# Who writes the final mask: VectorE before the hand-over, or ScalarE in front of each exponential

## The chip, the cores and the metric

One core of a Trainium2 chip runs the whole program. The metric is device time in microseconds of one execution; the kernel before took 3034.04 us (median of 3 runs, 3031.94 to 3041.01).

## The reference, cut to what matters

Four layers run one after the other on 2048 tokens of 128 features: linear attention, a mixture-of-experts feed-forward, the talking-heads attention that this change touches, and a second mixture of experts. The third layer, with 16 heads, 16 memory slots ahead of the 2048 keys, and a causal mask:

```python
dots = jnp.einsum('bhid,bhjd->bhij', q, k) * SCALE
dots = jnp.einsum('bhij,hk->bkij', dots, pre_proj)
dots = jnp.where(causal, NEG_INF, dots)
topk_vals = jax.lax.top_k(dots, K)[0]          # K = 64
thresh = topk_vals[..., -1:]
dots = jnp.where(dots < thresh, NEG_INF, dots)
attn = jax.nn.softmax(dots, axis=-1)
out = jnp.einsum('bhij,bhjd->bhid', attn, v)
```

Each row of scores keeps its 64 largest entries, all others get the weight zero.

## The kernel before, in words

The attention works on 64 groups `k`. A group is one tile of 128 queries (`t = k // 4`, 16 tiles) with four heads (`GU = 4`). Its rows are `n = 16 + 128 * (t + 1)` wide: 144 columns in the first four groups, 2064 in the last four. Scores stand in `S[:, k % 3, i, 0:n]`, in a ring of three groups (`NS = 3`), the mask in `F[:, i, 0:n]`, of which there is one copy only. Every engine runs its own list of instructions in order, and they meet at semaphores.

**VectorE**, per group: `pivots(k)` merges sorted lists to a pivot that lies close to the threshold (24 small operations and, beside them, `list_step(k + 1, ...)`, 64 MAX8 over the scores of the next group, L1106, four in each of 16 steps of `beside`), computes `negm` and `cutb` and raises `s_cut`. Then comes `memory_weights(k - 1)`, which waits for the exponentials of the group before and writes `Pm` from `F` and `S` (L1260). Then `below(k, i)` for four heads (L1155, L1157), and `threshold(k)`: it waits for ScalarE's counts (`s_cnt`), makes the threshold `thr`, judges whether a row is doubtful (L1228 to L1248), writes the masks of the four heads between these small steps (`mask`, L1176: 4.0 where the score lies below the threshold), reads the flag, skips the exact settlement `settle` in almost all groups, and raises `s_lose`. Before the first mask it waits until TensorE has read the masks of the group before (`s_tfill`, L1233).

**ScalarE**, in round `p`: `exponent(p - 1, i)` for four heads, in place in `S` (L543, waits for `s_lose`); the drains `drain_turn` of the first three transposed blocks (L550, a Relu from PSUM); `count_above(p, i)` for four heads (L536, waits for `s_cut`), with one further `drain_turn` behind each; the remaining `drain_turn`; `drain_rest(p - 1)`; and last `drain_scores(p + 2)`, which copies the scores of the group after next out of PSUM (L521). The exponentials of group `p` stand behind these copies in the list.

**TensorE**, in round `p`: `outputs(p - 2)`, `values(p - 1)` and `group_scores(p + 2)`. In `values`, `turn` transposes each block of exponentials (L807, waits for `s_prob` of its head) and subtracts the transposed mask in the same place of PSUM (L808); the Relu of the drain turns the difference into zero where the mask stands. `turn_memory` (L816) waits for `Pm`; `product` (L823) multiplies with the values.

```python
for p in range(NG):
    pivots(p)
    if p >= 1:
        memory_weights(p - 1)
    for i in range(GU):
        below(p, i)
    threshold(p)
```

Of the kernel before, what the change touches and what calls it, by code (L numbers as in the profile page):

```python
# [5 lines left out]
ALU = mybir.AluOpType  # L6
ACT = mybir.ActivationFunctionType
# [16 lines left out]
NS = 3  # L24
SC = 1024
BIG_ = 2.0 ** 90
# [7 lines left out]
GU = 4  # L34
# [11 lines left out]
def wide(t):  # L46

    return MEM + P * (t + 1)
# [114 lines left out]
def build(nc, out, x, Wqkv, bqkv, wi, bi, wo, bo0, loraA, loraB, gate_w, gate_b, Wq, Wkv, Wo, bo1, pre, mem_k, mem_v,  # L163
          ln_w, ln_b, router_w, gw1, uw1, dw1, shg, shu, shd):
    fills, ffills = plan_fills(), plan_ffn1()
    with ExitStack() as ctx:
# [3 lines left out]
        def sem(name):  # L170
            return ctx.enter_context(nc.semaphore(name))
# [27 lines left out]
        thr = sb("thr", [P, GU])  # L199
# [21 lines left out]
        sm = sb("sm", [P, 8, NT])  # L221
# [44 lines left out]
        WvZ = SA[:, 13184:15232].rearrange("p (c e n) -> p c e n", c=8, e=2)  # L266
        mvZ = SA[:, 15232:16256].rearrange("p (c e m) -> p c e m", c=8, e=2)
        mkS = SA[:, 2048:4096].rearrange("p (c k m) -> p c k m", c=8, k=H1)
        S = R[:, 0:NS * GU * WIDE].rearrange("p (r i n) -> p r i n", r=NS, i=GU)
        A = R[:, NS * GU * WIDE:(NS * GU + 2) * WIDE].rearrange("p (r n) -> p r n", r=2)  # L270
        F = sb("F", [P, GU, WIDE], BF16)
# [21 lines left out]
        s_dve = sem("s_dve")  # L293
# [21 lines left out]
        s_eight = sem("s_eight")  # L315
        s_lose = sem("s_lose")
        s_prob = sem("s_prob")
        s_pm = sem("s_pm")
        s_tfill, s_tdrain = sem("s_tfill"), sem("s_tdrain")
        s_pv = sem("s_pv")  # L320
# [13 lines left out]
        def turned(k):  # L334
            return turn_of["p", k, k // 4] + 1
# [77 lines left out]
        def _(act):  # L413
# [48 lines left out]
            n = fills.index("loraA_gate")  # L462
# [75 lines left out]

            def exponent(k, i):
                n = wide(k // 4)  # L540
                act.wait_ge(s_lose, k + 1)
                row = S[:, k % NS, i, 0:n]
                act.activation(row, row, ACT.Exp, bias=negm[:, k % 2, i:i + 1], scale=1.0 / LOW).then_inc(s_prob, 1)  # L543

            def drain_turn(k, j):
# [52 lines left out]
            for e in range(E0 + 1):  # L598
                for b in range(4):
                    for i in range(2):  # L600
                        k = (e * 4 + b) * 2 + i
# [320 lines left out]
        def _(dve):  # L922
            done = [0]

            def mark(ins):
                done[0] += 1
                ins.then_inc(s_dve, 1)
# [39 lines left out]
            for b in range(4):  # L967
                k = drained(("q", b))
# [11 lines left out]
            k = drained("kvsum")  # L980
# [21 lines left out]
            k = drained("logit0")  # L1002
# [93 lines left out]
            def list_step(k, first, count):  # L1096

                if k >= NG:
                    return  # L1100
                n = wide(k // 4)
                for m in range(first, first + count):
                    i, c = divmod(m, CH)
                    if c == 0:
                        dve.wait_ge(s_sdrain, last_slot(k, i) + 1)
                    mark(dve.max(cand[:, :, c, i], lists(S[:, k % NS, i, 0:n], n, c)))  # L1106

            def pivots(k):

                def beside(step, ins):
                    mark(ins)
                    stage = done[0]
                    list_step(k + 1, 4 * step, 4)
                    dve.wait_ge(s_dve, stage)
                    return step + 1

                dve.wait_ge(s_dve, done[0])
                mark(dve.tensor_reduce(top[:, :], cand[:, 0].rearrange("p l u -> p u l"), AX.X, ALU.max))  # L1119
                link(dve.tensor_scalar(W16[:, 0, :], cand[:, :, :, :].rearrange("p r l u -> p (r l u)"), 1.0 / LOW, -RANGE,  # L1120
                                       ALU.mult, ALU.max))
                flip, runs, step = 0, 8, 0
                while runs < TOPK:
                    inner = 8 * CH * GU // (2 * runs)
                    src = W16[:, flip, :].rearrange("p (r h n) -> p r h n", r=runs, h=2)
                    flip = 1 - flip
                    dst = W16[:, flip, :].rearrange("p (h r n) -> p h r n", h=2, r=runs)
                    mark(dve.tensor_tensor(dst[:, 0], src[:, :, 0, :], src[:, ::-1, 1, :], ALU.max))
                    step = beside(step, dve.tensor_tensor(dst[:, 1], src[:, :, 0, :], src[:, ::-1, 1, :], ALU.min))
                    d = runs // 2  # L1130
                    while d:
                        src = W16[:, flip, :].rearrange("p (r h n) -> p r h n", h=2, n=d * inner)
                        flip = 1 - flip
                        dst = W16[:, flip, :].rearrange("p (r h n) -> p r h n", h=2, n=d * inner)
                        mark(dve.tensor_tensor(dst[:, :, 0, :], src[:, :, 0, :], src[:, :, 1, :], ALU.max))  # L1135
                        step = beside(step, dve.tensor_tensor(dst[:, :, 1, :], src[:, :, 0, :], src[:, :, 1, :], ALU.min))  # L1136
                        d //= 2
                    runs *= 2
                src = W16[:, flip, :].rearrange("p (r h u) -> p r h u", h=2, u=GU)
                dst = W16[:, 1 - flip, 0:CUT * GU].rearrange("p (r u) -> p r u", u=GU)  # L1140
                beside(step, dve.tensor_tensor(dst, src[:, 0:CUT, 0, :], src[:, CUT - 1::-1, 1, :], ALU.max))
                link(dve.tensor_reduce(piv[:, :], dst.rearrange("p r u -> p u r"), AX.X, ALU.min))
                mark(dve.tensor_scalar(negm[:, k % 2, :], top[:, :], -1.0 / LOW, None, ALU.mult))
                link(dve.tensor_scalar(cutt[:, :], piv[:, :], -BIG_ * LOW * (1 - NEAR), BIG_ * LOW * SLACK,
                                       ALU.mult, ALU.add))
                link(dve.scalar_tensor_tensor(out=cutb[:, k % 2, :], in0=piv[:, :], scalar=-BIG_ * LOW * (1 + NEAR),
                                              in1=cutt[:, :], op0=ALU.mult, op1=ALU.max))
                dve.sem_inc(s_cut, 1)  # L1148
# [22 lines left out]
                                                in1=bob[:, 0:P - 1] if g == 0 and i == 0 else y, op0=ALU.mult,  # L1171
                                                op1=ALU.add)

            def mask(k, i):
                n = wide(k // 4)
                mark(dve.tensor_scalar(F[:, i, 0:n], S[:, k % NS, i, 0:n], thr[:, i:i + 1], 4.0, ALU.is_lt, ALU.mult))  # L1176

            def settle(k, i):

                n = wide(k // 4)  # L1180
                dve.tensor_reduce(doubts[:, 0, 0:1], doubt[:, i::GU], AX.X, ALU.max)
                dve.drain()
                dve.transpose(doubts[:, 1, :], doubts[:, 0, :])
                dve.drain()
                dve.tensor_reduce(flag[:, :], doubts[0:1, 1, :], AX.X, ALU.max)
                dve.drain()
                row, rest, m_ = S[:, k % NS, i, 0:n], A[:, 1, 0:n], r9[:, i, 1:9]
                with dve.If(dve.value_load(flag[0:1, 0:1], min_val=0, max_val=1) != 0):
                    for r in range(8):
                        dve.max(m_, rest if r else row)  # L1190
                        dve.drain()
                        if r < 7:
                            dve.match_replace(rest, m_, rest if r else row, 2 * FILL)
                            dve.drain()
                    dve.tensor_copy(thr[:, i:i + 1], m_[:, 7:8])
                    dve.drain()
                    dve.tensor_scalar(F[:, i, 0:n], row, thr[:, i:i + 1], 4.0, ALU.is_lt, ALU.mult)
                    dve.drain()

            def threshold(k):  # L1200
# [27 lines left out]
                    mark(dve.scalar_tensor_tensor(out=doubt[:, GU * g:GU * g + GU], in0=th[rows_g, :], scalar=0.0,  # L1228
                                                  in1=tie[rows_g, :], op0=ALU.is_equal, op1=ALU.max))
                judged = done[0]  # L1230
                if k:

                    dve.wait_ge(s_tfill, turned(k - 1))  # L1233
                mask(k, 0)
                dve.wait_ge(s_dve, judged)
                mark(dve.tensor_reduce(doubts[:, 0, 0:1], doubt[:, :], AX.X, ALU.max))
                judged = done[0]
                mask(k, 1)
                dve.wait_ge(s_dve, judged)
                mark(dve.transpose(doubts[:, 1, :], doubts[:, 0, :]))  # L1240
                judged = done[0]
                mask(k, 2)
                dve.wait_ge(s_dve, judged)
                mark(dve.tensor_reduce(flag[:, :], doubts[0:1, 1, :], AX.X, ALU.max))
                judged = done[0]
                mask(k, 3)
                dve.wait_ge(s_dve, judged)
                doubtful = dve.value_load(flag[0:1, 0:1], min_val=0, max_val=1)  # L1248
                with dve.If(doubtful != 0):
                    dve.drain()  # L1250
                    for i in range(GU):
                        settle(k, i)
                dve.wait_ge(s_dve, done[0])
                dve.sem_inc(s_lose, 1)  # L1254

            def memory_weights(k):
                dve.wait_ge(s_prob, GU * k + GU)
                if k:
                    dve.wait_ge(s_tfill, turn_of["m", k - 1, 0] + 1)
                dve.scalar_tensor_tensor(out=Pm[:, :, :], in0=F[:, :, 0:MEM], scalar=1.0, in1=S[:, k % NS, :, 0:MEM],  # L1260
                                         op0=ALU.is_lt, op1=ALU.mult).then_inc(s_pm, 1)

            list_step(0, 0, CH * GU)
            for p in range(NG):
                pivots(p)
                if p >= 1:
                    memory_weights(p - 1)
                for i in range(GU):
                    below(p, i)
                threshold(p)  # L1270
# [80 lines left out]
```

## Time and profile before

| | us | share of the span |
|---|---|---|
| median of the runs shown | 3034.04 | |
| profiled execution | 3029.58 | |
| its span | 3027.1 | |
| VectorE busy | 2415.8 | 80% |
| TensorE busy (matmul) | 2302.1 | 76% |
| ScalarE busy | 1414.6 | 47% |
| the 64 groups of attention, first pivot to the end of the last products | some 2440 | 81% |

The profile shows one execution. Busy times are shares of the whole span, over stages that differ: before 325 us and after 2770 us other layers run. Inside the attention the groups grow from 20.5 us at the start to about 54 us at the end, so what an operation costs has to be read by stretch. "Idle before" is the time in which an engine stood still ahead of a group of instructions, with the instruction that released it; "issue" is a pause for which the profile shows no releaser. DVE is VectorE, ACT is ScalarE, PE is TensorE.

### The profile page before, as it was taken

How to read it: one execution, taken by the hardware profiler on the slowest of the kernel's cores; microseconds unless marked ns; L12 is line 12 of the kernel's file. 1: busy time of each engine (PE TensorE's matmuls, PEld its weight loads, DVE VectorE, ACT ScalarE, POOL GpSimd, SP SyncE). 2: the span in 40 equal slices, each digit the busy share in tenths (PEclk: the TensorE clock that was granted, in tenths of full speed). 3: DMA queues.
4: the chain of work that ended last, by engine and by line, in shares of the span. 5: the costliest groups of instructions: out<-in, count | busy, mean ns of one | idle time of the engine just before them, and what ended most of it. 6: DMA issues, size and time to landing. Idle time of an engine off the chain costs nothing.

```text
span 3027.1 us, 34365 instructions
## 1 busy us (share of the span) xinstructions
PE 2302.1 (76%) x10182; PEld 1328.8 (44%) x10182; DVE 2415.8 (80%) x9392; ACT 1414.6 (47%) x2143; POOL 5.2 (0%) x43
## 2 busy tenths in 40 slices
PE   6696545657767757778888888988984888884897
PEld 3554323333434424444444444544542545442564
DVE  2506688889888988989899999999998988884445
ACT  1121223444445435555565666666663666652221
POOL 0000000000000000000000000000000000000000
PEclk7798667777878878899998999999997999987898
DMA  2000000000000000000000000000000000001000
GB/s 59 1 0 1 1 1 1 1 1 1 2 1 1 1 1 1 1 1 1 1 1 1 1 1 1 1 1 1 1 1 1 1 1 1 1 1 49 1 1 14
DMA packets 15509, 12.20 MB, mean 4 GB/s; under 512 B 6892, under 2 KB 13686, under 8 KB 15222
## 3 DMA queue, kind: packets, MB, share of 16 engines
q1 hardware_dynamic: 11184, 6.82, 0.9%
q10 hardware_dynamic: 4038, 2.37, 0.3%
q14 instruction: 206, 1.69, 0.2%
q8 instruction: 81, 1.33, 0.2%
HBM read 8.14 MB, written 1.05 MB: 3 GB/s over the span
## 4 chain that ended last, share of the span: by engine, by line
DVE 53%; PE 30%; ACT 8%; issue 7%; DVEq 2%; ACTq 0%
DVE cand L1106 13%; DVE R L1155 7%; DVE r L1157 7%; PE bank L823 6%; PE bank L791 6%; PE bank L903 4%; DVE W L1136 4%; DVE F L1176 4%; DVE W L1135 4%; ACT R L543 4%; PE bank L807 3%; ACT R L536 3%; PE bank L911 2%; DVE WP L1170 2%; PE bank L808 1%
## 5 line engine op out<-in xcount | busy, mean ns | idle before, releaser
L823 PE MATMUL bank<-WP,Y 128*128 128x512 f32 x1088 | 685.4, 718 | 152.0 <-ACT WP L550 151.2
L807 PE MATMUL bank<-ident,R 128*128 128x128 f32 x2176 | 524.0, 315 | 248.8 <-ACT R L543 246.6
L1106 DVE MAX8 cand<-R 128x8 f32<-128x12 f32 (+15 forms) x4096 | 642.6, 226 | 5.3 <-ACT R L521 4.2
L791 PE MATMUL bank<-hT,qT 128*128 128x512 f32 (+3 forms) x1280 | 533.1, 555 | 37.3 <-ACT R L521 22.2
L807 PEld LDWEIGHTS bank<-ident,R 128*128 128x128 f32 x2176 | 346.2, 159 | 465.6 <-issue 214.7
L550 ACT ACTIVATE WP<-bank 128x512 f32<-128x512 f32 x544 | 320.8, 594 | 369.8 <-PE bank L808 368.6
L808 PE MATMUL bank<-nidentb,F 128*128 128x128 bf16 x2176 | 466.3, 240 | 0.0
L536 ACT ACTIVATE R<-R,cutb 128x144 f32<-128x144 f32 (+15 forms) x256 | 310.2, 1212 | 294.1 <-DVEq L1148 292.5
L521 ACT ACTIVATE R<-bank 128x1024 f32<-128x1024 f32 (+7 forms) x384 | 290.5, 774 | 278.6 <-PE bank L791 168.3
L1155 DVE SCALAR_TENSOR_TENSOR R<-R,r 128x144 f32<-128x144 f32 (+15 forms) x256 | 350.3, 1368 | 9.2 <-DVE r L1154 0.2
L543 ACT ACTIVATE R<-R,negm 128x144 f32<-128x144 f32 (+15 forms) x256 | 289.8, 1205 | 123.9 <-DVEq L1254 123.7
L791 PEld LDWEIGHTS bank<-hT,qT 128*128 128x128 f32 x1280 | 232.2, 198 | 262.3 <-issue 191.8
L1157 DVE MAX8 r<-R 128x8 f32<-128x144 f32 (+15 forms) x256 | 335.8, 1312 | 8.8
L808 PEld LDWEIGHTS bank<-nidentb,F 128*128 128x128 bf16 x2176 | 257.1, 118 | 142.9 <-issue 142.9
L823 PEld LDWEIGHTS bank<-WP,Y 128*128 128x128 f32 x1088 | 192.4, 221 | 205.7 <-ACT WP L550 194.4
L1136 DVE TENSOR_TENSOR W<-W 128x256 f16<-128x256 f16 x768 | 220.4, 287 | 0.0
L1176 DVE TENSOR_SCALAR F<-R,thr 128x144 bf16<-128x144 f32 (+15 forms) x256 | 196.9, 770 | 27.1 <-PE bank L808 25.3
L1135 DVE TENSOR_TENSOR W<-W 128x256 f16<-128x256 f16 x768 | 211.9, 276 | 1.2 <-DVE cand L1106 0.8
L1119 DVE TENSOR_REDUCE top<-cand 128x4 f32<-128x64 f32 x64 | 17.2, 269 | 128.6 <-issue 118.0
L816 PE MATMUL bank<-ident,Pm 128*64 128x128 f32 x64 | 20.3, 317 | 130.9 <-DVE Pm L1260 130.9
L903 PE MATMUL bank<-R 128*128 128x512 f32 x256 | 115.1, 593 | 0.7 <-ACT R L587 0.7
L587 ACT ACTIVATE R<-bank 128x512 f32<-128x512 f32 x76 | 45.4, 597 | 144.4 <-PE bank L903 140.2
(225 smaller groups left out, 2164.1 us busy)
## 6 DMA issues: line engine op xcount, KB each, us to landing
R<-in_L_attn_Wkv ACTq DMA_DIRECT2D x2, 512.0 KB, 8.0
R<-in_L_ffn_gate_w SPq DMA_DIRECT2D x1, 1024.0 KB, 7.7
R<-in_L_ffn_up_w SPq DMA_DIRECT2D x1, 1024.0 KB, 10.3
out<-X SPq DMA_DIRECT2D x1, 1024.0 KB, 5.1
R<-in_L_attn_Wq ACTq DMA_DIRECT2D x1, 512.0 KB, 6.1
WP<-in_L_attn_Wo ACTq DMA_DIRECT2D x1, 512.0 KB, 10.5
R<-in_L_ffn_wi SPq DMA_DIRECT2D x1, 256.0 KB
R<-in_L_ffn_wo SPq DMA_DIRECT2D x1, 256.0 KB
```

The lines of the kernel that those rows point to most:

```text
L536: act.activation(A[:, 0, 0:n], S[:, k % NS, i, 0:n], ACT.Sign, bias=cutb[:, k % 2, i:i + 1], scale=BIG_, accum_out=cnt[:, k % 2, i:i + 1]) ...
L543: act.activation(row, row, ACT.Exp, bias=negm[:, k % 2, i:i + 1], scale=1.0 / LOW).then_inc(s_prob, 1)
L550: act.activation(PT[:, b % 4, :], bank[4 + n % 2], ACT.Relu).then_inc(s_tdrain, 1)
L791: last = pe.matmul(to, qT[:, k % 2, i, :], hT[:, a:b], start=True, stop=b < n, skip_group_check=True)
L807: pe.transpose(to[:, P * i:P * i + P], S[:, k % NS, i, blk], ident[:, :])
L808: last = pe.matmul(to[:, P * i:P * i + P], F[:, i, blk], nidentb[:, :], start=False, stop=True, skip_group_check=True)
L823: pe.matmul(bank[6], Y[:, j, :], PT[:, (blocks_before(k) + j) % 4, :], start=(j == 0), stop=(j == k // 4))\
L1106: mark(dve.max(cand[:, :, c, i], lists(S[:, k % NS, i, 0:n], n, c)))
L1135: mark(dve.tensor_tensor(dst[:, :, 0, :], src[:, :, 0, :], src[:, :, 1, :], ALU.max))
L1136: step = beside(step, dve.tensor_tensor(dst[:, :, 1, :], src[:, :, 0, :], src[:, :, 1, :], ALU.min))
L1155: link(dve.scalar_tensor_tensor(out=A[:, 1, 0:n], in0=row, scalar=r9[:, i, 0:1], in1=row, op0=ALU.is_gt, op1=ALU.subtract, reverse1=True))
L1157: dve.max(r9[:, i, 1:9], A[:, 1, 0:n]).then_inc(s_eight, 1)
```

## The change

VectorE no longer writes the masks. It keeps the small steps of the judgement, and at the end of `threshold` writes the four thresholds times 2^90 into `thrb`, in one of two halves. ScalarE gets a second activation per head in `exponent`: a Relu over the whole row, with that threshold as bias and -2^90 as scale, so that `F` is zero where the score reaches the threshold and very large where it doesn't. It waits for its own Relu (`s_mask`), since the exponential overwrites the row that the Relu reads. Ahead of the first head it waits for `s_pm` and for TensorE's reading of the old masks. `memory_weights(k - 1)` moves from behind `pivots(k)` into it: step 7 in groups below 8, one step later every eight groups, step 14 of the 16 (0 to 15) from group 56 on. The exact settlement no longer rewrites its mask.

```diff
             def exponent(k, i):
                 n = wide(k // 4)
-                act.wait_ge(s_lose, k + 1)
                 row = S[:, k % NS, i, 0:n]
+                if i == 0:
+                    act.wait_ge(s_lose, k + 1)
+                    if k:
+                        act.wait_ge(s_pm, k)
+                        act.wait_ge(s_tfill, turned(k - 1))
+                act.activation(F[:, i, 0:n], row, ACT.Relu, bias=thrb[:, k % 2, i:i + 1], scale=-BIG_).then_inc(s_mask, 1)
+                act.wait_ge(s_mask, GU * k + i + 1)
                 act.activation(row, row, ACT.Exp, bias=negm[:, k % 2, i:i + 1], scale=1.0 / LOW).then_inc(s_prob, 1)
...
                     list_step(k + 1, 4 * step, 4)
+                    if k >= 1 and step == 7 + k // 8:
+                        memory_weights(k - 1)
                     dve.wait_ge(s_dve, stage)
...
-            def mask(k, i):
-                n = wide(k // 4)
-                mark(dve.tensor_scalar(F[:, i, 0:n], S[:, k % NS, i, 0:n], thr[:, i:i + 1], 4.0, ALU.is_lt, ALU.mult))
...
                     dve.tensor_copy(thr[:, i:i + 1], m_[:, 7:8])
-                    dve.drain()
-                    dve.tensor_scalar(F[:, i, 0:n], row, thr[:, i:i + 1], 4.0, ALU.is_lt, ALU.mult)
                     dve.drain()
...
                 judged = done[0]
-                if k:
-
-                    dve.wait_ge(s_tfill, turned(k - 1))
-                mask(k, 0)
                 dve.wait_ge(s_dve, judged)
                 mark(dve.tensor_reduce(doubts[:, 0, 0:1], doubt[:, :], AX.X, ALU.max))
                 judged = done[0]
-                mask(k, 1)
...
-                dve.wait_ge(s_dve, done[0])
-                dve.sem_inc(s_lose, 1)
+                dve.tensor_scalar(thrb[:, k % 2, :], thr[:, :], BIG_, None, ALU.mult).then_inc(s_lose, 1)
...
                 pivots(p)
-                if p >= 1:
-                    memory_weights(p - 1)
                 for i in range(GU):
                     below(p, i)
```

## Rows read from the trace of the kernel before

**Rows 1.** The page: busy time by engine, and two rows of the 40 slices.

```profile
PE 2302.1 (76%) x10182; PEld 1328.8 (44%) x10182; DVE 2415.8 (80%) x9392; ACT 1414.6 (47%) x2143; POOL 5.2 (0%) x43
PE   6696545657767757778888888988984888884897
DVE  2506688889888988989899999999998988884445
```

**Rows 2.** Groups by line, 1174 to 2770 us: mean ns, then idle before and releaser.

```profile
L807 PE MATMUL bank<-ident,R 128*128 128x128 f32 x1728 | 397.6, 305 | 158.4 <-ACT R L543 157.4
L536 ACT ACTIVATE R<-R,cutb 128x1168 f32<-128x1168 f32 (+8 forms) x140 | 223.6, 1597 | 62.5 <-DVEq L1148 62.5
L543 ACT ACTIVATE R<-R,negm 128x1040 f32<-128x1040 f32 (+8 forms) x144 | 216.6, 1580 | 35.2 <-DVEq L1254 35.1
L1176 DVE TENSOR_SCALAR F<-R,thr 128x1168 bf16<-128x1168 f32 (+8 forms) x140 | 141.4, 1011 | 26.1 <-PE bank L808 25.3
L816 PE MATMUL bank<-ident,Pm 128*64 128x128 f32 x36 | 9.8, 273 | 0.0
```

**Rows 3.** Groups by line, 325 to 1174 us.

```profile
L536 ACT ACTIVATE R<-R,cutb 128x144 f32<-128x144 f32 (+7 forms) x116 | 86.6, 746 | 231.6 <-DVEq L1148 229.9
L543 ACT ACTIVATE R<-R,negm 128x144 f32<-128x144 f32 (+6 forms) x112 | 73.1, 723 | 88.6 <-DVEq L1254 88.6
L1176 DVE TENSOR_SCALAR F<-R,thr 128x144 bf16<-128x144 f32 (+7 forms) x116 | 55.5, 479 | 0.9
L816 PE MATMUL bank<-ident,Pm 128*64 128x128 f32 x28 | 10.4, 373 | 130.9 <-DVE Pm L1260 130.9
```

**Rows 4.** Chain that ended last, in order of time: start us, us, what.

```profile
2589.59 7.73 ACT R L543 x4
...
2642.74 7.73 ACT R L543 x4
```

**Rows 5.** Timeline of ScalarE, group 60: start, us, instruction, idle before.

```profile
2588.67 1.02 ACT L521 ACTIVATE R<-bank 128x1024 f32<-128x1024 f32 x1 [0.75 <-PE bank L793]
...
2597.98 0.60 ACT L550 ACTIVATE WP<-bank 128x512 f32<-128x512 f32 x1 [0.67 <-PE bank L808]
```

**Rows 6.** Timeline of TensorE: behind the late settlement, and beside rows 5.

```profile
2327.17 0.45 PE L807 MATMUL bank<-ident,R 128*128 128x128 f32 x1 [28.11 <-ACT R L543]
...
2335.46 0.27 PE L807 MATMUL bank<-ident,R 128*128 128x128 f32 x1
...
2591.74 0.30 PE L807 MATMUL bank<-ident,R 128*128 128x128 f32 x1 [0.97 <-ACT R L543]
...
2595.46 0.48 PE L807 MATMUL bank<-ident,R 128*128 128x128 f32 x1 [1.52 <-ACT R L543]
...
2597.36 0.47 PE L807 MATMUL bank<-ident,R 128*128 128x128 f32 x1 [1.32 <-ACT R L543]
...
2599.02 2.02 PE L823 MATMUL bank<-WP,Y 128*128 128x512 f32 x2
...
2601.84 1.08 PE L823 MATMUL bank<-WP,Y 128*128 128x512 f32 x2
```

**Rows 7.** Timeline of ScalarE, groups 9 and 10.

```profile
570.48 2.19 ACT L543 ACTIVATE R<-R,negm 128x400 f32<-128x400 f32 x4 [5.75 <-DVEq L1254]
...
583.89 0.63 ACT L536 ACTIVATE R<-R,cutb 128x400 f32<-128x400 f32 x1 [5.64 <-DVEq L1148]
```

**Rows 8.** Timeline of VectorE, groups 60 and 61.

```profile
2571.05 1.29 DVE L1176 TENSOR_SCALAR F<-R,thr 128x2064 bf16<-128x2064 f32 x1 [4.43 <-PE bank L808]
...
2578.77 0.27 DVE L1119 TENSOR_REDUCE top<-cand 128x4 f32<-128x64 f32 x1 [2.56 <-issue]
...
2598.56 0.16 DVE L1144 TENSOR_SCALAR cutt<-piv 128x4 f32<-128x4 f32 x1
2598.76 0.16 DVE L1146 SCALAR_TENSOR_TENSOR cutb<-piv,cutt 128x4 f32<-128x4 f32 x1
```

**Rows 9.** Groups by line, whole span: the loads of ScalarE's tables at L428.

```profile
L428 ACT ACT_TABLE_LOAD x5 | 6.4, 1283 | 14.2 <-issue 14.1
```

More of the change, by code:

```diff
@@ L268, in build @@
         mkS = SA[:, 2048:4096].rearrange("p (c k m) -> p c k m", c=8, k=H1)
+        thrb = sm[:, 0, 0:2 * GU].rearrange("p (a i) -> p a i", a=2)
         S = R[:, 0:NS * GU * WIDE].rearrange("p (r i n) -> p r i n", r=NS, i=GU)
@@ L317, in build @@
         s_prob = sem("s_prob")
+        s_mask = sem("s_mask")
         s_pm = sem("s_pm")
@@ L1241, in threshold @@
                 judged = done[0]
-                mask(k, 2)
                 dve.wait_ge(s_dve, judged)
@@ L1245, in threshold @@
                 judged = done[0]
-                mask(k, 3)
                 dve.wait_ge(s_dve, judged)
```

## The prediction

> **What bounds the kernel now.** I read the page first. Overall VectorE is busy 80%, TensorE 76% and ScalarE 47%; in the slices VectorE stands at 8 or 9 tenths through the whole attention, and TensorE climbs beside it from 5 to 8 and 9 [rows 1]. By these shares VectorE is the bound and ScalarE has room. That reading is true for the first half only. What decides is who waits for whom, by stretch.
>
> In the early stretch (325 to 1174 us, groups 0 to 28) ScalarE stands idle 88.6 us ahead of its exponentials until VectorE raises `s_lose`, and 231.6 us ahead of its counts until VectorE raises `s_cut`; VectorE waits for nobody ahead of its masks (0.9 us in all), and TensorE waits 130.9 us for `Pm` [rows 3]. VectorE sets the pace.
>
> In the late stretch (1174 to 2770 us, groups 29 to 63) it turns round. TensorE waits 157.4 us for the exponentials and not at all for `Pm`. ScalarE's wait for `s_cut` has shrunk to 62.5 us, its wait for `s_lose` to 35.1 us, and VectorE waits 25.3 us for TensorE ahead of its masks [rows 2]. The timeline of group 60 shows why: ScalarE's last copy of scores starts at 2588.67 and takes 1.02 us, and the four exponentials follow with no gap at all, 2589.59 to 2597.32, although VectorE had been done with the masks for more than ten microseconds (its next pivot started at 2578.77) [rows 4, 5, 8]. TensorE meanwhile does one transposition per finished exponential and waits again, and gets going only behind the fourth, at 2597.36 [rows 6]. The chain that ended last holds these pieces of four exponentials, 7.73 us each, with 53.15 us from one to the next [rows 4]. So late groups run in a serial ring: exponentials on ScalarE, transpositions, products and new scores on TensorE, their copies on ScalarE, next exponentials. VectorE runs beside that ring.
>
> **The change, part by part.**
>
> *Relu on ScalarE, late stretch.* It is put exactly into that ring, in front of each exponential, and TensorE has nothing else in its list to do meanwhile. The trace has no Relu of this shape. The nearest row is the exponential over the same rows with the same kind of bias; the count, another function over the same rows, has nearly the same mean (1597 against 1580 ns), so I take the exponential's busy time again: 216.6 us for 144 activations [rows 2]. The wait on its own semaphore takes away the overlap of neighbours. Four exponentials of 400 columns take 2.19 us back to back, about 0.52 us apart; a count of the same width takes 0.63 us [rows 7]. A start behind a wait for the end of such an activation comes at 0.63 and a little, so about 0.13 us later than without, and 144 of them add 18.7 us. Bounds of that gap: zero, if the overlap stays, to 0.20, the whole distance of two dependent small operations on VectorE [rows 8]; that is 0 to 29 us. Added to the ring: 235 us.
>
> Not all of it lengthens the ring, since the ring has slack that it would use up first. ScalarE's 62.5 us of waiting for `s_cut` [rows 2] is time in which the ring waited for VectorE. With longer groups the pivots are there earlier. But `memory_weights(k - 1)` now stands inside `pivots(k)` and waits for the last exponential of the group before, and behind it come one to six further steps and the tail of `pivots`: in group 61 `pivots` takes 20.1 us from L1119 to L1146 for 16 steps and its tail [rows 8], so one step and the tail come to some 3 us, and four to six of the shorter steps of narrower groups to some 6. ScalarE first has three blocks to drain in that time, which TensorE hands over until about 2602, some 5 us behind the last exponential [rows 6]. I leave 8 us of the wait standing and take 54 as absorbed. Of the 35.1 us behind `s_lose`, most stands at one group with a settlement on VectorE, behind which TensorE had paused 28.11 us [rows 6], and the remaining 7 or so at the end; by my reading the first shrinks by about 6, since VectorE is further ahead of the ring, and the second goes: 13 absorbed. Late stretch: 235 - 54 - 13 = +168 us.
>
> *Masks off VectorE.* Late, it saves 141.4 us of busy time and 25.3 us of waiting [rows 2], and I cost both at nothing, since the ring doesn't wait for VectorE there. What then hides VectorE is the ring; VectorE will wait at L1260. Early, the saving counts. But of four masks three stood between the small steps of the judgement and hid their latencies. Now these are bare: three steps at 0.20 us, the distance of two dependent small operations [rows 8], and about 0.05 for the new `thrb`, 0.65 us per group. The reading of the flag behind the last step took longer than the fourth mask before and stays as it is. So 29 groups save three quarters of 55.5 [rows 3] = 41.6, less 29 x 0.65 = 18.9, which is 22.8. I choose to give the last five of them nothing (5 x 1.5 = 7.5 us less), since the ring takes over just behind them and grows earlier than before. Early stretch: -15 us.
>
> *Relu on ScalarE, early.* 73.1 + 112 x 0.13 = 88 us more work lies beside VectorE's; cover is the 231.6 and 88.6 us that ScalarE stood idle [rows 3]. *`memory_weights` moved.* The same instruction, 0.23 us, once per group; TensorE's 130.9 us of waiting for `Pm` [rows 3] mostly goes, and is worth nothing while VectorE sets the pace. What it can cost: behind L1260 are queued the rest of `pivots`, `s_cut`, and so ScalarE's counts. Early, four pairs take 8 x 0.72 = 5.8 us in the mean [rows 3], and the step comes at the middle of `pivots`, so I cost the wait at nothing; if it came 1 us too late in each of 29 groups, 29 us. *ScalarE's new waits* for `s_pm` and `s_tfill` are met already, because its own drains of the group before stood behind the same events: nothing. *The settlement* without its four masks: two groups, under 5 us.
>
> *The pause ahead of L1119.* The 2.56 us of "issue" stand behind the branch over the settlement [rows 8]. The block gets a little shorter; whether more or fewer groups pay, the trace doesn't tell. I keep it, with 20 us either way.
>
> *A rule of the skill.* The masks take 1011 ns on VectorE where an activation over the same rows takes 1580 [rows 2], so the work grows by more than half as it moves. The Trainium skill, "ScalarE: Activation LUTs", Rules for kernel authors, says to use VectorE, not ScalarE, for relu, since VectorE is up to about three times faster per element in bf16. It speaks against this change; here the input is f32, and the trace gives a ratio of 1.6. By a factor of three the estimate for the late masks would be 424 us instead of 235; the row decides.
>
> **The sum.** 168 - 15 = +153 us on the profiled execution of 3029.6 us, which gives 3183. The median of the runs shown is 4.5 us higher, and I put the forecast at 3185 us.
>
> **The rivals.**
>
> *VectorE bounds throughout, the masks' going is a gain.* For it: the slices show VectorE at 9 tenths to the end [rows 1]. Then three quarters of all masks, 0.75 x 196.9 = 148, less 64 x 0.65 = 42, and the 25 us of waiting go: 131 us faster, 2903 us. It decides from the point where the exponentials start on `s_lose` and not behind ScalarE's copies. Against it: no gap ahead of the exponentials of group 60 [rows 4, 5], and only 35.1 us of waiting for `s_lose` in 144 exponentials [rows 2].
>
> *The ring's slack is larger than I read.* TensorE might make up the delay, since fewer of its turns would meet the counts on ScalarE. If half of the 168 us were made up, the time is 3100. A case within 0.3% would need all of it.
>
> *The change doesn't do what it says:* Relu and exponential would reload tables between them. A load takes 1.28 us [rows 9]; eight per group make over 600 us. But the drains' Relu at L550 follows the last exponential after 0.67 us, a wait for TensorE and no load [rows 5]. 1%.
>
> **Chances.** Forecast 72%; slack larger 10%; clock 8%; VectorE bound 6%; about no change 3%; tables 1%. The range runs from 3105 to 3250: it takes in the bounds of the self-wait, the pause and most of the slack. About 0.3% is what a measurement of this kernel can tell from no change. Faster by over 0.3%: 0.07; within: 0.03; slower: 0.90.
>
> **What would show it.** Right: in late groups the four pairs of Relu and exponential take 16 us on ScalarE, directly behind L521; TensorE's idle ahead of L807 grows from 158 to about 370 us; VectorE's busy time falls by about 190 us and it stands waiting at L1260; the late groups take some 60 us. Early groups get up to 1 us shorter. Wrong: if late exponentials start on `s_lose`, if the Relu takes clearly more or less than the exponential, or if the part of the ring that isn't exponentials (45 us in group 60) changes.

## The result, and the profile after

The changed kernel takes 3160.15 us (median of 4 runs, 3156.91 to 3162.37) against 3034.38 us before (median of 4 runs): a ratio of 1.041, 95% interval 1.0391 to 1.0429. It is 126 us slower. The profiled execution has a span of 3159.0 us against 3027.1.

The overview page of the changed kernel: busy time by engine, and two rows of the 40 slices, answering to [rows 1].

```profile
PE 2303.4 (73%) x10182; PEld 1332.7 (42%) x10182; DVE 2254.5 (71%) x9198; ACT 1719.4 (54%) x2399; POOL 5.2 (0%) x43
PE   6697555667777577777777877878685778765797
...
DVE  2406688888988888878787877777679776763445
```

VectorE has lost 161 us of busy time and ScalarE has gained 305. TensorE's busy time is the same, spread over a longer span. VectorE no longer stands at 9 tenths towards the end but at 6 and 7: it is the engine that waits now.

Where the time went is told by two stretches with the same 29 and 35 groups as before. Groups by line of the changed kernel, 325 to 1153 us (groups 0 to 28), answering to [rows 3]; the columns are busy us, mean ns of one, idle time before and its releaser:

```profile
L815 PE MATMUL bank<-ident,R 128*128 128x128 f32 x448 | 130.5, 356 | 147.7 <-ACT R L551 147.7
L538 ACT ACTIVATE R<-R,cutb 128x144 f32<-128x144 f32 (+7 forms) x116 | 86.6, 747 | 130.4 <-DVEq L1158 128.8
L549 ACT ACTIVATE F<-R,sm 128x144 bf16<-128x144 f32 (+6 forms) x112 | 81.0, 723 | 67.1 <-DVE sm L1250 67.1
L824 PE MATMUL bank<-ident,Pm 128*64 128x128 f32 x28 | 8.6, 305 | 11.8 <-DVE Pm L1256 11.7
```

L549 is the new Relu, L551 the exponential, L538 the count, L1250 the new `thrb` (a part of the tile `sm`, under whose name it stands in the views), L1256 the memory weights. `DVEq L1158` is VectorE's raising of `s_cut`. ScalarE still waits for VectorE here, only less. The first pivot of group 29 starts 815.5 us behind that of group 0; before it was 844.8. The early stretch has gained 29 us.

The same view from 1153 to 2905 us (groups 29 to 63), answering to [rows 2]:

```profile
L815 PE MATMUL bank<-ident,R 128*128 128x128 f32 x1728 | 402.4, 308 | 370.2 <-ACT R L551 370.2
L551 ACT ACTIVATE R<-R,negm 128x1040 f32<-128x1040 f32 (+8 forms) x144 | 228.7, 1588 | 4.7
L549 ACT ACTIVATE F<-R,sm 128x1040 bf16<-128x1040 f32 (+8 forms) x144 | 226.9, 1576 | 23.5 <-DVE sm L1250 23.5
L538 ACT ACTIVATE R<-R,cutb 128x1168 f32<-128x1168 f32 (+8 forms) x140 | 223.8, 1599 | 3.4 <-DVEq L1158 3.3
L824 PE MATMUL bank<-ident,Pm 128*64 128x128 f32 x36 | 9.8, 273 | 0.0
L1256 DVE SCALAR_TENSOR_TENSOR Pm<-F,R 128x64 f32<-128x64 bf16 x36 | 8.0, 224 | 247.3 <-ACT R L551 247.3
```

TensorE's wait for exponentials has grown from 158 to 370 us. ScalarE's wait for `s_cut` ahead of its counts has gone from 62.5 to 3.4 us: the ring has used up its slack. And VectorE stands still for 247.3 us ahead of the memory weights. That large number is a symptom. VectorE waits because the ring is longer, and the experiments below show that its place in the list costs nothing here (`mask_only`), as long as it stands late enough in the pivots (`step7`).

One late group in order of time. Timeline of ScalarE in group 59 of the changed kernel (start us, duration, instruction; in brackets idle before), answering to [rows 5]:

```profile
2636.11 1.02 ACT L523 ACTIVATE R<-bank 128x1024 f32<-128x1024 f32 x1 [0.75 <-PE bank L801]
2637.03 1.90 ACT L549 ACTIVATE F<-R,sm 128x1936 bf16<-128x1936 f32 x1
2638.96 1.91 ACT L551 ACTIVATE R<-R,negm 128x1936 f32<-128x1936 f32 x1
2640.78 1.89 ACT L549 ACTIVATE F<-R,sm 128x1936 bf16<-128x1936 f32 x1
...
2650.18 1.91 ACT L551 ACTIVATE R<-R,negm 128x1936 f32<-128x1936 f32 x1
```

TensorE beside it, answering to [rows 6]:

```profile
2641.02 0.30 PE L815 MATMUL bank<-ident,R 128*128 128x128 f32 x1 [2.80 <-ACT R L551]
2644.66 0.47 PE L815 MATMUL bank<-ident,R 128*128 128x128 f32 x1 [3.29 <-ACT R L551]
...
2652.14 0.47 PE L815 MATMUL bank<-ident,R 128*128 128x128 f32 x1 [3.16 <-ACT R L551]
...
2653.80 1.74 PE L831 MATMUL bank<-WP,Y 128*128 128x512 f32 x2
2655.38 0.27 PE L815 MATMUL bank<-ident,R 128*128 128x128 f32 x1
```

And VectorE: the thresholds are handed over at 2619.41, 18 us before ScalarE looks at them, and then it waits at L1256 for the last exponential, which ends at 2652.09.

```profile
2619.41 0.17 DVE L1250 TENSOR_SCALAR sm<-thr 128x4 f32<-128x4 f32 x1 [3.52 <-issue]
...
2652.12 0.23 DVE L1256 SCALAR_TENSOR_TENSOR Pm<-F,R 128x64 f32<-128x64 bf16 x1 [9.59 <-ACT R L551]
```

The block in front of TensorE lasts from 2637.03 to 2652.09, 15.1 us; in the kernel before the same group took 7.3 us, and its pieces stand in the chain that ended last (start us, us, what):

```profile
2536.75 7.30 ACT R L543 x4
...
2589.59 7.73 ACT R L543 x4
```

From the end of that block to the start of the next it took 2589.59 - 2544.05 = 45.5 us before. The same chain of the changed kernel has the first Relu of group 60 at 2696.75, 44.7 us behind 2652.09:

```profile
2696.75 2.02 ACT F L549
```

So in this group the rest of the ring is nearly what it was, and the block in it has doubled.

### The profile page after: what moved, and what is told of

It reads as the page before. It is cut to its first block, busy times and chain, and to the rows that moved or that the text cites. A ratio compares the mean times of both kernels' runs of the same rounds, so it can differ in the third digit from the quotient of the medians.

```text
span 3159.0 us, 34424 instructions
## 1 busy us (share of the span) xinstructions
PE 2303.4 (73%) x10182; PEld 1332.7 (42%) x10182; DVE 2254.5 (71%) x9198; ACT 1719.4 (54%) x2399; POOL 5.2 (0%) x43
## 4 chain that ended last, share of the span: by engine, by line
PE 42%; DVE 29%; ACT 21%; issue 7%; DVEq 2%; ACTq 0%
PE bank L799 10%; PE bank L831 10%; ACT R L551 7%; DVE cand L1114 7%; ACT F L549 7%; PE bank L815 5%; PE bank L911 4%; ACT R L538 4%; DVE R L1165 3%; DVE r L1167 3%; DVE W L1146 2%; PE bank L816 2%; ACT R L523 2%; DVE W L1145 2%; PE bank L919 2%
## 5 line engine op out<-in xcount | busy, mean ns | idle before, releaser
L815 PE MATMUL bank<-ident,R 128*128 128x128 f32 x2176 | 532.9, 318 | 517.9 <-ACT R L551 517.9
L831 PE MATMUL bank<-WP,Y 128*128 128x512 f32 x1088 | 653.9, 688 | 55.3 <-ACT WP L558 53.5
L799 PE MATMUL bank<-hT,qT 128*128 128x512 f32 (+3 forms) x1280 | 540.2, 559 | 115.0 <-ACT R L519 91.2
L523 ACT ACTIVATE R<-bank 128x1024 f32<-128x1024 f32 (+7 forms) x384 | 290.5, 774 | 286.4 <-PE bank L799 168.3
L538 ACT ACTIVATE R<-R,cutb 128x144 f32<-128x144 f32 (+15 forms) x256 | 310.5, 1213 | 133.8 <-DVEq L1158 132.0
L549 ACT ACTIVATE F<-R,sm 128x144 bf16<-128x144 f32 (+15 forms) x256 | 307.9, 1203 | 90.6 <-DVE sm L1250 90.6
L551 ACT ACTIVATE R<-R,negm 128x144 f32<-128x144 f32 (+15 forms) x256 | 311.0, 1215 | 8.3
L831 PEld LDWEIGHTS bank<-WP,Y 128*128 128x128 f32 x1088 | 184.0, 212 | 108.1 <-ACT WP L558 97.0
L1146 DVE TENSOR_TENSOR W<-W 128x256 f16<-128x256 f16 x768 | 216.5, 282 | 0.8 <-issue 0.8
L1145 DVE TENSOR_TENSOR W<-W 128x256 f16<-128x256 f16 x768 | 209.0, 272 | 0.4
L1256 DVE SCALAR_TENSOR_TENSOR Pm<-F,R 128x64 f32<-128x64 bf16 x64 | 13.7, 215 | 247.3 <-ACT R L551 247.3
L1250 DVE TENSOR_SCALAR sm<-thr 128x4 f32<-128x4 f32 x64 | 10.9, 170 | 163.6 <-issue 163.6
L595 ACT ACTIVATE R<-bank 128x512 f32<-128x512 f32 x76 | 45.4, 597 | 144.5 <-PE bank L911 140.2
```

Source lines behind the costliest of these rows:

```text
L523: act.activation(S[:, k % NS, i, MEM + SC * c:MEM + SC * c + w], src[:, 0:w], ACT.Copy)\
L538: act.activation(A[:, 0, 0:n], S[:, k % NS, i, 0:n], ACT.Sign, bias=cutb[:, k % 2, i:i + 1], scale=BIG_, accum_out=cnt[:, k % 2, i:i + 1]) ...
L549: act.activation(F[:, i, 0:n], row, ACT.Relu, bias=thrb[:, k % 2, i:i + 1], scale=-BIG_).then_inc(s_mask, 1)
L799: last = pe.matmul(to, qT[:, k % 2, i, :], hT[:, a:b], start=True, stop=b < n, skip_group_check=True)
L815: pe.transpose(to[:, P * i:P * i + P], S[:, k % NS, i, blk], ident[:, :])
L831: pe.matmul(bank[6], Y[:, j, :], PT[:, (blocks_before(k) + j) % 4, :], start=(j == 0), stop=(j == k // 4))\
```

## The experiments

Comparisons are ratios to the kernel before in the same session, with 95% intervals. Where a time is split, "early" is from the first pivot of group 0 to that of group 29 and "late" from there to the end of the span: 844.8 and 1852.5 us before, 815.5 and 2005.3 us after.

### Each part of the change alone

`weights_only`: the kernel before, with the memory weights inside the pivots.

```diff
                     list_step(k + 1, 4 * step, 4)
+                    if k >= 1 and step == 7 + k // 8:
+                        memory_weights(k - 1)
...
                 pivots(p)
-                if p >= 1:
-                    memory_weights(p - 1)
```

> The kernel before with one part of the change alone: the memory weights are taken inside the pivots, the masks stay on VectorE. Theory (ring: in late groups the exponentials, TensorE's transpositions, products and scores and ScalarE's copies follow each other serially, and the Relu lengthened that ring): 3034 us, between 3025 and 3043, since neither the ring nor VectorE's work changes; TensorE's wait of 131 us for the memory weights shrinks to under 20 us and is worth nothing. Rival (weights: VectorE, held at the memory weights in front of its signal for the counts, is what made the changed kernel slower): at least half of the 126 us, 3097 us or more.

Measured: 3032.84 us, ratio 0.9992 (0.9982 to 1.0002): no difference. TensorE's early wait for the memory weights falls from 130.9 to 39.1 us, less far than I expected, and is worth nothing, as expected.

`mask_only`: the changed kernel, with that edit undone.

> The changed kernel with the memory weights back in their old place behind the pivots, so the other part alone. Ring: as slow as the changed kernel, 3160 us, between 3150 and 3168; VectorE then waits below the signal for the counts instead of above it. Weights: back to 3097 us or less.

Measured: 3159.69 us, ratio 1.0413 (1.0398 to 1.0427), the changed kernel's time. The whole loss belongs to the masks, and the 247 us that VectorE waits at L1256 are no cause.

### What the Relu costs, by its width and number

`narrow_relu`: the mask of all but the 16 memory columns is left out, so this kernel does not compute the reference. `F` is set to zero once at the start, by a line that the diff leaves out.

```diff
-                act.activation(F[:, i, 0:n], row, ACT.Relu, bias=thrb[:, k % 2, i:i + 1], scale=-BIG_).then_inc(s_mask, 1)
+                act.activation(F[:, i, 0:MEM], S[:, k % NS, i, 0:MEM], ACT.Relu, bias=thrb[:, k % 2, i:i + 1], scale=-BIG_).then_inc(s_mask, 1)
```

> The changed kernel with a Relu over the 16 memory columns only; the mask of all other columns is left out (zero), so it measures what the width of the Relu costs. Ring: the late Relus shrink from 226.9 us to some 144 x 0.3 = 43 us, 184 us out of the ring, until VectorE catches it: 2990 us, between 2965 and 3010, so faster than before by over 1%. Rival (the Relu lies beside other work; the loss comes from waits and order, which stay): 3130 us or more.

Measured: 2992.84 us, ratio 0.9854 (0.9836 to 0.9871). Every wait in the attention and the order of the list are those of the changed kernel; only the width is different, and 167 us are gone. 166 of them are late (1839.1 us), and 1.3 early (814.2 us). So the width of the Relu is free in the early groups. In the late ones the Relus got 184 us shorter (226.9, less 144 at 295 ns), and 90% of that came off the time.

```profile
L549 ACT ACTIVATE F<-R,sm 128x16 bf16<-128x16 f32 x256 | 75.4, 295 | 73.9 <-DVE sm L1251 73.7
```

The row is from the groups by line of this kernel, whole span: 295 ns for 16 columns, against 1576 in the mean of the late ones of full width.

`double_relu`: each Relu done twice.

```diff
-                act.activation(F[:, i, 0:n], row, ACT.Relu, bias=thrb[:, k % 2, i:i + 1], scale=-BIG_).then_inc(s_mask, 1)
-                act.wait_ge(s_mask, GU * k + i + 1)
+                for r in range(2):
+                    act.activation(F[:, i, 0:n], row, ACT.Relu, bias=thrb[:, k % 2, i:i + 1], scale=-BIG_).then_inc(s_mask, 1)
+                    act.wait_ge(s_mask, 2 * (GU * k + i) + r + 1)
```

> The changed kernel with every Relu done twice, each awaited. Ring: in the late stretch 144 x (1.58 + 0.13) = 246 us more, less some 8 of slack at the settlement; in the early stretch the longer ScalarE block passes the step at which VectorE takes the memory weights, some 55 us over groups 4 to 28: 3453 us, between 3420 and 3480. Rival (ScalarE's work lies beside others' and only the first Relu's wait counts): 3200 us or less.

Measured: 3421.54 us, ratio 1.1269 (1.1252 to 1.1286), just inside the range. Late it costs 2239.0 - 2005.3 = 234 us where I expected 238. Early it costs 26 us (841.6 against 815.5) where I expected 55: VectorE's early wait at the memory weights rises from nothing to 25.3 us, so it stops there less than I had made it.

### The wait for its own Relu

`masks_first`: four Relus, then four exponentials, so that no exponential waits for the Relu just ahead.

```diff
                 if i == 0:
...
+                    for j in range(GU):
+                        act.activation(F[:, j, 0:n], S[:, k % NS, j, 0:n], ACT.Relu, bias=thrb[:, k % 2, j:j + 1],
+                                       scale=-BIG_).then_inc(s_mask, 1)
-                act.activation(F[:, i, 0:n], row, ACT.Relu, bias=thrb[:, k % 2, i:i + 1], scale=-BIG_).then_inc(s_mask, 1)
                 act.wait_ge(s_mask, GU * k + i + 1)
```

> The changed kernel with all four Relus of a group in front of its four exponentials. No exponential then waits for the Relu just in front of it. Ring: the self-wait, 12.1 us of longer exponentials and 4.7 us of idle time in the late stretch, goes out of the ring: 3143 us, between 3138 and 3150. Rival (TensorE profits from every head that comes early, so pairs are better than blocks): TensorE has its first three transpositions of a group later; if they counted, about 1 us in each of 36 groups, the time would not fall: 3160 us or more.

Measured: 3143.14 us, ratio 1.0357 (1.0343 to 1.0372), 16 to 17 us less than the changed kernel, nearly all of it late (1989.3 us). That TensorE gets its first heads later costs nothing that shows; it waits for the fourth anyway.

### Early and late apart

`hybrid28` lets ScalarE write the masks in groups 0 to 27 and VectorE, as before, from group 28 on; `late_only28` does the reverse.

```diff
+SWITCH = 28
...
+                if k < SWITCH:
+                    act.activation(F[:, i, 0:n], row, ACT.Relu, bias=thrb[:, k % 2, i:i + 1], scale=-BIG_).then_inc(s_mask, 1)
+                    act.wait_ge(s_mask, GU * k + i + 1)
...
+            def mask(k, i):
+                if k >= SWITCH:
+                    n = wide(k // 4)
+                    mark(dve.tensor_scalar(F[:, i, 0:n], S[:, k % NS, i, 0:n], thr[:, i:i + 1], 4.0, ALU.is_lt, ALU.mult))
```

> Masks by ScalarE in groups 0 to 27, by VectorE as before in groups 28 to 63; memory weights inside the pivots throughout. Ring: the early saving of the changed kernel stays (29.4 us from the first pivot to that of group 29 by the two profiles, some 27 of it before group 28) and the late loss goes: 3010 us against 3037, between 3003 and 3018. Rival (the early saving is an accident of instruction pauses, or ScalarE's extra work costs early too): within 0.3% of before, 3028 us or more.

> The reverse: masks by VectorE in groups 0 to 27, by ScalarE from group 28 on. Ring: before plus the late loss of 153 us by the two profiles, 3190 us, between 3180 and 3198: slower than the changed kernel. Rival (the loss is spread over all groups): between before and after, 3150 us or less.

Measured: `hybrid28` 3005.43 us, ratio 0.9905 (0.9889 to 0.9920), early 816.3 and late 1851.2 us; `late_only28` 3191.12 us, ratio 1.0517 (1.0501 to 1.0533), early 840.2 and late 2010.6 us. The one change is a gain of 1% up to group 27 and a loss of 5% from group 28 on. Both effects add up to what was measured for the whole. `hybrid28` beats both kernels. Group 28 is the only switch point that was tried.

### Exponentials out of the ring

`among44` goes on from `hybrid28`. From group 44 on the thresholds are mostly there well before the ring comes round (in `hybrid28` 4 to 13 us before, but for two groups), so three of the four exponentials are done among the copies of scores, while TensorE still computes.

```diff
             def drain_scores(k):
+                ready = k - 2 if k - 2 >= AMONG else None
+                gone = 0
                 for name in plan_slots():
                     if name[1] == k and name[0] != "q" or name[0] == "q" and name[1] == k + 1:
                         drain_slot(name)
+                        if ready is not None and name[0] == "s" and name[3] == slots(k // 4) - 1 and name[2] >= 1:
+                            exponent(ready, gone)
+                            gone += 1
...
-                    for i in range(GU):
+                    for i in range(3 if AMONG <= p - 1 and p + 1 < NG else 0, GU):
                         exponent(p - 1, i)
```

> As hybrid28, and from group 44 on ScalarE takes three of the four exponentials of a group among its copies of the scores of the group after next, one behind each of the last three heads, while TensorE still computes scores. That takes exponentials out of the ring. Ring: TensorE's pause ahead of the transpositions shrinks by some 5 us per group; VectorE, with 46 to 51 us of own work per group, becomes the bound again at about the same level, so only its wait for TensorE ahead of the masks (25 us) and a little goes: 2985 us, between 2975 and 3000. Rival (the exponentials delay the copies, TensorE waits there instead): 3010 us or more, no better than hybrid28.

Measured: 2983.58 us, ratio 0.9827 (0.9813 to 0.9840), the fastest of all. The late stretch falls from 1851.2 to 1827.6 us. TensorE's waits for exponentials in the whole run fall by 75 us against `hybrid28` (307.6 us, groups by line), of which 24 us reach the end. Between the pivots of groups 44 and 63 TensorE's idle time as a whole falls only from 140.6 to 135.4 us: it waits 46 us more for the copies of scores and 25 more at the products, so the rival had a part of it right. What got shorter is VectorE's idle time, from 58.5 to 37.8 us, about what the stretch gained; of its 914 us VectorE is idle in 4%, so it sets the pace again. The longest waits of `among44` (engine, line, releaser: us in total, times, longest):

```profile
PE bank L823 <- ACT R L559: 232.3, 189, 23.5
ACT R L545 <- DVEq L1166: 223.6, 60, 10.9
```

L559 is its exponential, L545 its count: ScalarE waits for `s_cut` 60 times, 223.6 us in all; in `hybrid28` it was 48 times and 184.5 us.

### The step at which the weights are taken

`step7` takes the memory weights at step 7 in all groups.

```diff
-                    if k >= 1 and step == 7 + k // 8:
+                    if k >= 1 and step == 7:
```

> The changed kernel with the memory weights taken at step 7 of the pivots in every group, not later as the groups grow. VectorE waits there for the last exponential, so its signal for the counts comes eight steps and the tail of the pivots behind it, some 8.6 us in group 28 to 11 us in group 60, where ScalarE could start counting after some 5. Ring: 4 to 6 us more of waiting for that signal per late group, of which the first 1.5 us are free by the groups of the kernel before, and beyond which the ring loses the wait and up to a fifth more, since TensorE's clock falls again in it: some 190 us over 36 late groups, and some 18 us in groups 8 to 27: 3370 us, between 3300 and 3400. Rival (the step at which the weights are taken matters little, as VectorE has time): 3160 us, within 1%.

Measured: 3325.39 us, ratio 1.0951 (1.0933 to 1.0970). The place of that one small instruction is not harmless after all: taken too early in a late group it holds the pivots behind it, and with them `s_cut`. The loss is 162 us late (2166.9 us), 28 less than I expected, and 6 us early (821.7 us), 12 less. From the groups by line of this kernel, late stretch:

```profile
L538 ACT ACTIVATE R<-R,cutb 128x1168 f32<-128x1168 f32 (+8 forms) x140 | 223.3, 1595 | 141.0 <-DVEq L1158 141.0
L1256 DVE SCALAR_TENSOR_TENSOR Pm<-F,R 128x64 f32<-128x64 bf16 x36 | 8.1, 225 | 432.6 <-ACT R L551 432.6
```

ScalarE's wait for `s_cut` rises from 3.4 to 141.0 us. Group by group, 28 to 59, the wait grows by 127 us and the ring by 150, 1.18 times as much. Summed from the instruction and clock records of the two traces over the 32 intervals between one block and the next, TensorE stands idle 97 us longer and its own work, the same instructions, takes 53 us longer. The part of that work at the 1.2 GHz level grows from 131.6 to 250.4 us; half of the difference, 59 us by this estimate, is what the lower level costs. One such group in its timeline:

```profile
2008.24 1.08 PE L831 MATMUL bank<-WP,Y 128*128 128x512 f32 x2
2012.93 1.12 PE L831 MATMUL bank<-WP,Y 128*128 128x512 f32 x2 [2.93 <-ACT WP L558]
2014.98 2.08 PE L831 MATMUL bank<-WP,Y 128*128 128x512 f32 x2
2017.90 1.08 PE L831 MATMUL bank<-WP,Y 128*128 128x512 f32 x2
```

The pair right behind the pause of 2.93 us takes 1.12 us, the next one 2.08 and the one after it 1.08 again: the granted clock has fallen from 2.4 to 1.2 GHz a second time in the group, at 2014.22, and rises at 2017.63.

## Why the prediction was right, point by point

**The sign and the mechanism** were right. I read two regimes out of one kernel, the later one a serial ring through ScalarE and TensorE with VectorE beside it. The changed profile shows the ring as forecast: Relu directly behind L523, a block of 15 us at 1936 columns, 370 us of idle time ahead of the transpositions where I had written about 370, VectorE waiting at the memory weights. `narrow_relu` and `double_relu` show that the width of the Relu is the cause, `mask_only` and `weights_only` that the moved weights are not.

**The size** was 25 us too high, 3185 against 3160.15, inside the range. (The terms themselves, 3183 and the 4.5 us of the median, come to 3187.) Two terms carry that, and by the profiles they are 15 and 14 us too high. A third part belongs to neither: the stretch ahead of the first pivot took 329.7 us before and 338.2 after, and it lies between 330 and 341 us in the eleven profiles with and without the change, so it is scatter.

*Late, 168 us forecast, 152.8 measured* (2005.3 - 1852.5). The work added was about right: the blocks from the first Relu to the last exponential are 233.6 us longer than the old ones, summed over the 36 groups 28 to 63, where I had 235. The self-wait was right as well: I had 18.7 us, and `masks_first` gives back 16. What I mis-sized is the slack absorbed, some 79 us instead of 67: 71 in groups 28 to 59 and 8 in the last ones, where ScalarE had waited for VectorE.

From the end of one block to the start of the next, groups 28 to 59 took 1227.2 us before and 1156.4 after, 70.8 less. ScalarE's wait for `s_cut` in them fell by 59 us, 5 more than I had, and its wait at the settlement by 4.4. The other 7 us stand behind no wait of ScalarE: I had taken a microsecond of wait for at most a microsecond of ring. TensorE's records over the same 32 intervals split the 70.8 us in another way: its idle time went from 127.6 to 76.5 us, 51 less, and its own work from 1099.7 to 1079.9, 20 less. The part of the work at the 1.2 GHz level went from 163.0 to 131.6 us; half of the difference, 16 us by this estimate, is what the higher level gave back. In the profiles of `weights_only` and `mask_only` the same part is 167.5 and 142.0 us, which would give 13. The kernel before shows what more a long wait costs. Timeline of its TensorE in group 29:

```profile
1220.81 1.08 PE L823 MATMUL bank<-WP,Y 128*128 128x512 f32 x2
1228.57 2.07 PE L823 MATMUL bank<-WP,Y 128*128 128x512 f32 x2 [6.01 <-ACT WP L550]
1231.72 1.61 PE L823 MATMUL bank<-WP,Y 128*128 128x512 f32 x2
1233.84 1.08 PE L823 MATMUL bank<-WP,Y 128*128 128x512 f32 x2
```

ScalarE waited 6.77 us for `s_cut` in that group, TensorE 6.01 us for the drain behind it, and came out of it at half the clock; the rest of the ring in this group was 8.2 us longer than in the changed kernel. Not every wait costs more than its length: 1.85 us in group 31 cost nothing (27.97 against 28.19 us), 2.15 us in group 43 cost 1.74. Once the pivots were no longer late, most of these second slow pieces went too, and `step7` brings them back. No run changes the clock by itself; its share is read from the records.

*Early, 15 us forecast, 29.4 measured.* From the end of the last judgement (L1228, now L1232) to the next pivot VectorE took 147.1 us over 29 groups before and 120.2 after, 26.9 less. I had 22.8, of which I took 7.5 away again for the last five groups, by choice; they saved 4.2, and the first 24 saved 22.7 where 15.3 were left. Part of that shift is the pause of "issue" shown below, which one group fewer of the first 24 has and two more of the last five. For the rest, the small steps without the masks seem to cost less than the 0.65 us per group that I had put on them; no run measures them by themselves. Moving the weights into the pivots took away another 2.6 us: `pivots` grew by 3.2 us in 29 groups, and the stretch from there to the judgement, where the weights had stood, shrank by 5.8. Group 9 before and group 10 after, VectorE:

```profile
564.88 0.70 DVE L1228 SCALAR_TENSOR_TENSOR doubt<-thr,tie 32x4 f32<-32x4 f32 x4
...
570.53 0.27 DVE L1119 TENSOR_REDUCE top<-cand 128x4 f32<-128x64 f32 x1 [3.23 <-issue]
```

```profile
592.57 0.70 DVE L1232 SCALAR_TENSOR_TENSOR doubt<-thr,tie 32x4 f32<-32x4 f32 x4
593.73 0.17 DVE L1242 TENSOR_REDUCE flag<-doubts 1x1 int32<-1x32 f32 x1
595.10 0.17 DVE L1250 TENSOR_SCALAR sm<-thr 128x4 f32<-128x4 f32 x1 [1.20 <-issue]
```

These two also show the pause of "issue" that one group has and another hasn't: a changed group takes 1.9 to 2.2 us from judgement to pivot without it and 3.9 to 4.5 with it, and 18 of the 29 have it where 17 had it before, the group with a settlement counted in both. "Some 20 us either way" was more room than it needed.

**The rivals.** "VectorE bounds throughout" holds in the early groups alone: `hybrid28` gets 28.5 us of the 131 that it promised (early stretch, 844.8 to 816.3). "Larger slack" was right in direction, by 12 us and not by 84. "The clock falls further" did not come: the mean granted clock went from 0.859 to 0.835, but the slow piece behind the block is no longer than it was (the first pair of products 1.74 us against 2.02 before, full speed from 2655.38, 3.3 us behind the last exponential), and what is added is half clock while TensorE waits: inside the blocks of groups 28 to 59 it grew from 38.5 to 242.3 us, while TensorE's work at half clock between the blocks fell. "Tables": one load stands at L551 in the whole run, as one stood at L543 before. The Trainium skill, "ScalarE: Activation LUTs", Rules for kernel authors, prefers VectorE for relu, and the trace agrees in direction: a late mask took 1011 ns on VectorE [rows 2] and 1576 as a Relu on ScalarE, a ratio of 1.6. Yet in groups 0 to 27 the dearer engine was the right one, because it was idle.

**A sign that held only at the place it was read.** I had written that a change of the rest of the ring (45 us in group 60) would speak against me. In group 60 it is 45.3 us against 45.4; in the narrower groups it shrank, by the 70.8 us above.

**A number that was off** without effect: VectorE's busy time fell by 161 us and not by 190. The small steps that had overlapped with the masks now count by themselves, and `thrb` is new.

## What to carry to other kernels

Work moved to the engine with the lowest busy share is only free if it doesn't stand in front of what the next engine waits for. Follow one period of a late and of an early stage by hand, from the end of one block to its next start: if the block begins directly behind another copy on its engine and the follower waits for nothing else, nearly each microsecond there is a microsecond of the period. A kernel whose stages grow can have two bounds, and the same edit can be a gain in one and a loss in the other; then switch by stage, and take the blocks apart (`among44`), instead of choosing for all.

## What the runs showed of the hardware that was not expected

A pause of TensorE in the middle of its work can cost more than its length. In 32 late groups of `step7` 127 us more of ScalarE's waiting for `s_cut` made the ring 150 us longer: 97 us are TensorE's idle time, and 53 are its own work, slower because more of it (250.4 us instead of 131.6) ran at the lower clock. Around a pause of 2.93 us in `step7`, and behind one of 6.01 us in the kernel before, pairs of products took 2.08 and 2.07 us instead of 1.08. Behind the block of Relus and exponentials, which had doubled to 15 us, the slow piece was no longer than behind 7 us.

An activation that waits for the one ahead of it on the same engine starts about 0.11 us later than one that doesn't: `masks_first` got back 16 us over 144 of them.
